# Four step tables of a four-layer transformer kernel in another order, with the waits that this order needs

## The reference

```python
mod = silu(cond) @ W_mod + b_mod                 # shift, scale, gate, twice
q, k, v = split((LN(x) * (1 + sc_a) + sh_a) @ W_qkv + b_qkv)
x = x + gate_a * (attend(q, k, v) @ W_proj + b_proj)     # self attention, 256 keys
x = x + attend(LN(x) @ W_q, context @ W_kv) @ W_cproj    # cross attention, 120 keys
x = x + gate_m * (gelu((LN(x) * (1 + sc_m) + sh_m) @ W_1) @ W_2)   # MLP, 1024 wide
```

## Time and profile before

| | before |
|---|---|
| median of three runs | 2457.98 us |
| profiled execution, its own time | 2459.47 us |
| its span, first to last instruction | 2457.7 us |
| TensorE (PE) busy | 2394.8 us, 97% |
| VectorE (DVE) busy | 1875.6 us, 76% |
| ScalarE (ACT) busy | 1263.5 us, 51% |
| GpSimd (POOL) busy | 466.9 us, 19% |
| chain that ended last | PE 91%, DVE 5%, ACT 1%, issue 1%, DMA 1% |

### The profile page before, as it was taken

The page is one execution under the profiler, slowest core; times in us unless marked ns, Lnnn a source line. Parts: engine busy times, 40 slices in busy tenths (PEclk is TensorE's granted clock), DMA queues, the critical chain, the costliest instruction groups (busy, mean ns, idle before and its releaser), DMA issues.

```text
span 2457.7 us, 93436 instructions
## 1 busy us (share of the span) xinstructions
PE 2394.8 (97%) x41326; PEld 1616.7 (66%) x41326; DVE 1875.6 (76%) x3532; ACT 1263.5 (51%) x1810; POOL 466.9 (19%) x510
## 2 busy tenths in 40 slices
...
GB/s 214 133 113 61 99 86 78 78 88 85 80 84 84 91 93 76 93 89 72 70 88 60 85 78 55 88 88 70 94 108 60 106 70 76 100 60 89 85 40 39
DMA packets 143669, 209.27 MB, mean 85 GB/s; under 512 B 14978, under 2 KB 75588, under 8 KB 143268
## 3 DMA queue, kind: packets, MB, share of 16 engines
...
...
## 4 chain that ended last, share of the span: by engine, by line
PE 91%; DVE 5%; issue 1%; ACT 1%; DMA 1%; SPq 0%; POOL 0%; POOLq 0%; DVEq 0%; ACTq 0%
PE ring L1220 38%; PE ring L1216 13%; PE o_acc L1380 12%; PE score L1327 11%; PE score L1349 9%; PE ring L1174 4%; PE score L1354 3%; DVE row_max_F L1008 3%; DVE row_max_G L1008 2%; ACT probs L1147 1%; DMA gate_now_P<-gate_rows 0%; SPq L693 0%; PE ring L1256 0%; DMA q_F<-q_parts 0%; DMA k_G<-k_parts 0%
## 5 line engine op out<-in xcount | busy, mean ns | idle before, releaser
L1147 ACT ACTIVATE probs<-score 120x2048 f32<-120x2048 f32 (+1 forms) x320 | 601.6, 1880 | 302.2 <-PE score L1354 273.5
L1008 DVE TENSOR_REDUCE row_max_F<-score 128x8 f32<-128x2048 f32 x192 | 438.6, 2285 | 88.8 <-PE score L1327 86.2
L1158 ACT ACTIVATE h_t<-ring,cols 128x256 f32<-128x256 f32 x384 | 160.6, 470 | 415.5 <-PE ring L1220 289.3
L1008 DVE TENSOR_REDUCE row_max_G<-score 128x16 f32<-128x1920 f32 x128 | 276.2, 2158 | 65.4 <-PE score L1327 65.4
L1220 PE MATMUL ring<-x_t_E,w_fc 128*32 128x256 f32 x4736 | 279.6, 380 | 0.0
L1030 DVE STREAM_TRANSPOSE o_turned<-o_acc 128x512 f32<-128x512 f32 x224 | 159.4, 712 | 127.7 <-PE o_acc L1380 127.2
L1220 PE MATMUL ring<-w_fc,h_t 128*32 128x256 f32 x3680 | 215.4, 380 | 0.0
L1220 PEld LDWEIGHTS ring<-x_t_E,w_fc 128*32 128x32 f32 x4736 | 149.0, 110 | 100.2
L1380 PE MATMUL o_acc<-probs,v_self 128*17 128x256 f32 x3072 | 203.8, 383 | 0.4 <-DVE o_turned L1030 0.4
L817 POOL TENSOR_TENSOR x<-x,gated 128x512 f32<-128x512 f32 x48 | 61.2, 1274 | 612.1 <-DVE gated L1049 611.8
L1349 PE MATMUL score<-q_F,k_F 32*128 32x256 f32 x3072 | 166.1, 302 | 9.0 <-ACT probs L1147 4.5
...
## 6 DMA issues: line engine op xcount, KB each, us to landing
k_F<-k_parts SPq DMA_DIRECT2D x192, 256.0 KB, 2.5
q_G<-q_parts SPq DMA_DIRECT2D x128, 256.0 KB, 2.6
k_G<-k_parts SPq DMA_DIRECT2D x256, 120.0 KB, 2.1
...
```

The lines of the kernel that those rows point to most:

```text
L1008: nc.vector.tensor_reduce(dst, src, AX.X, ALU.max).then_inc(row_max_ready[r].sem, 1)
L1147: nc.scalar.activation(probs[v % 2][0:keys, :, :], score[0:keys, :].rearrange("p (h q) -> p h q", h=2 * GROUPS), ACT.Exp, scale=SCALE).the ...
L1158: last = nc.scalar.activation(h_t[:, c, :], ps[:, c % 2 * NT:(c % 2 + 1) * NT], ACT.Gelu_apprx_tanh, bias=col(m, "fc1", c))
```

## The change

The four tables get another order. No step is added or taken away, no table takes a turn more or less, and no instruction changes its shape but for the products that change between untiled and four column tiles, since the steps around them changed. Two waits are added, because two orders are now possible that were not before: ACT waits for the Q, K and V products of the job before (not V alone) before it overwrites `x_t_P`, and PE waits for `x_t_P` before V too (until now V always stood behind a step that had waited).

```diff
 TURN = """
-F.S1 E.H1 P.V
-F.S2 E.H2 P.LN P.V.d
-F.S3 A.PR A.PR.d F.X E.H3
-G.S0 F.M B.PR R.C B.PR.d
...
+F.S1 E.H2 R.C P.LN P.gld
+F.S2 f.O1 f.PV3 P.V
+F.S3 F.X E.H3 A.PR P.V.d
+G.S0 c.ld A.PR.d F.M B.PR
...
 WITH_L1 = """
-1G.T0 R.N P.Q.d E.F21a G.M p.N
-1G.T1 1G.PV0 e.N 1G.O0 1R.KV R.RES
-F.T0 1G.PV1 1G.O1 E.F21b
+1G.T0 E.F21a P.K.d R.N G.M e.N R.A
+1G.T1 P.RES P.Q.d 1G.PV0 E.F21b p.N
+F.T0 1G.O0 1G.PV1 1R.KV
...
 START = """
-F0.T2 W0.v2 F0.PV1 P2.Q.d F1.X Z2.ZG F1.M P0.gld
+F1.S2 Z2.ZA F0.M P0.gld P2.Q W0.proj Z2.ZL Z2.ZS1
...
@@ block.scalar, step LN
                     if r == "P":
+                        q_psum[r].wait_before(act, m, n)
+                        k_psum.wait_before(act, m, n)
                         v_psum.wait_before(act, m, n)
@@ block.tensor, step V
                     if n == 0:
                         pe.wait_ge(w_v_loaded, full_done(m))
+                    pe.wait_ge(x_t_ready[r].sem, x_t_ready[r].after(m, n))
```

More of the change, by code:

```diff
@@ L49 @@
 TURN = """
-F.S0 f.O1 f.PV3 E.H0
-F.S1 E.H1 P.V
-F.S2 E.H2 P.LN P.V.d
-F.S3 A.PR A.PR.d F.X E.H3
-G.S0 F.M B.PR R.C B.PR.d
[L55 to L61, removed]
+F.S0 E.H0 E.H1
+F.S1 E.H2 R.C P.LN P.gld
+F.S2 f.O1 f.PV3 P.V
+F.S3 F.X E.H3 A.PR P.V.d
+G.S0 c.ld A.PR.d F.M B.PR
```

139 lines of the change are left out of this document (72 added, 67 removed).

## The result

The changed kernel takes 2462.58 us, the median of 18 runs (2458.76 to 2466.24). The kernel before, measured with it, takes 2458.17 (18 runs, 2456.30 to 2460.32). The ratio is 1.0016, its 95% interval 1.0010 to 1.0023: slower by 2.5 to 5.7 us, which is real but for the most part under the 4.9 us that counted as "slower" in the prediction. Of the kernels further down, `v2_early`, `best3` and `fx_pad` each had one execution that took 1.9 to 3.3 times as long as the others; it is counted in their medians and not in their ratios.

A forecast was written before the change was run, and what follows sets the result against it. PE was taken to bound the long middle, with idle time to gain only in the beginning. Terms 5.5 + 0.2 + 2.2 - 2.6 + 0.8 = +6.1 us on 2459.47 gave 2465.6, for a median 2464; range 2454 to 2472.

The forecast's parts named there:

- TURN, +5.5: 25 turns of `TURN`: +0.22 us each from PE's own work and waiting, +5.5 us in all (+2.5 to +9).
- edit 1: TURN: `R.C` leaves the interval behind `G.S0`; PE's own work +0.07 us a turn, plus a 0.09 us wait.
- The price of 1.98 for `B.PR`: TURN, `G.S0` interval: without `R.C`, untiled `B.PR` is followed by row tiles and takes 1.98 us, not 1.73.
- edit 2: TURN: new order of `R.LN`, `F21b`, `E.LN` before `F.T2`; 2.80 against 2.75 us, taken as +0.06 a turn.
- `G.PV0`: TURN: it moves by an interval, at a cost taken as 0 us, bounds -0.1 and +0.1.
- the thin covers: TURN: two covers under 0.1 us, as for PE's `F.T3`; taken as 0. Failing every turn: 2469, chance 0.15.
- Turns 3 to 5, +2.2: Turn 4: `F21b` leaves the `F.T0` to `F.T1` interval, PE idles, +1.9 us; with small shifts +2.2 (0 to +4.5).
- START, -2.6: First score step to turn 3: gate wait gone -2.4, other -0.5, later first score step +0.3; -2.6 us (-8.5 to +1.5).
- `P0.gld`'s early place on SP: START: the gate load stands four score steps earlier on SP, so DVE's wait at the first `A.PR` goes, some 2.4 us.
- `F.X` short in every job: `F.X`'s adding operation at 192 ns, not 1276, giving DVE 1.1 us a turn; pays nothing by itself.
- TAIL, +0.8: TAIL: two intervals fall under their need and others lose a little, +0.8 us (-0.5 to +2).
- The two intervals under their need: TAIL: `F15.S2` with one product, 2.5 against 3.15 us, and `G13.S1` with `KV` alone, 2.8 against 3.38.

The follow-up runs named there:

- v2_early: The kernel before with one START load, `W0.v2` (384 KB with its bias), moved to the beginning: 2454.71 us, ratio 0.9986.
- best3: The changed kernel with the old TURN, `E.F21b` behind `F.T0` in turn 4 and `P.Q` behind `F.T0` in turn 3: 2454.15 us, ratio 0.9980.
- fx_pad: The changed kernel with eight additional small DVE operations inside `F.X` in turns 22 to 46: 2461.53 us, ratio 1.0011.
- gld_late: The changed kernel with `P0.gld` moved back behind `F0.O0` in START, four score steps later: one run of 2459.67 us.
- fx_long: The changed kernel with `A.PR` and `A.PR.d` put ahead of `F.X` in TURN: 2486.12 us, ratio 1.0114.

## Why the prediction was right, and where its steps were not

The forecast, slightly slower, came out, with 2462.6 for 2464. That it came so near is luck in part. Measured in the two traces its terms add up to +2.3 us and not to +6.1: the loss in `TURN` was put 2.5 too high, that in the last turn 1.8, and the gain in `START` 1.1. Of the signs it named, the turn of 45.3 us, the short `F.X`, the 2.96 us with a hole in turn 4 and the first `A.PR` without a gate wait are there; turn 3 begins 1.5 us earlier and not 2 to 3.

- **TURN, +5.5, measured +3.0.** What held: there was no gain to be had from waits, and the `G.S0` interval lost its cover. The split was wrong. The prediction let edit 1 cost 0.07 of PE's own work and 0.09 of waiting. In the traces it costs PE no work, and 0.11 us of time because of two intervals that stand at their need. The `G.S0` interval needs 3.44 and not the 3.38 of the earlier trace rows (in turn 3 of before it takes 3.44 too, with 1.97 of waiting in it), so taking `R.C` out of it saved nothing; and the interval that took `R.C` in had 0.11 to spare for its 0.21, which the step left out. The price of 1.98 for `B.PR` in front of row tiles was misread: that interval of the earlier trace rows begins with an F `S` step at 691.42, so it is 3.15 long, which is its need, and 0.1 or more of the 1.98 is waiting.

```profile
691.42 0.75 PE L1327 MATMUL score<-k_F,q_F 32*128 32x256 f32 x16
```

  Where nothing waits, an untiled product takes 1.82 in front of row tiles (turn 4 of after, 199.50 to 201.32) and 1.72 in front of transposes (200.70 to 202.42 in before), and two transposes 0.32 (202.42 to 202.74 in before) and 0.22 (199.28 to 199.50 in after). So the way to row tiles costs 0.10 behind either. (Both are read in front of `T` steps. In front of an `S` step the product takes 1.87 in `fx_pad`, in an interval at its need, so a little of that can be waiting.) The rule of the Trainium skill that a change of mode drains TensorE ("TensorEngine Tiling (Array Packing)", Key Properties) would have made edits 1 and 2 free at one price for all changes. The trace agrees for edit 1. It disagrees for edit 2: the `LN` order cost 0.05 to 0.06, as the prediction said. `G.PV0` cost nothing, and the thin covers held. In sum 0.15, where 0.22 was forecast.
- **Turn 35**, which no term contains, gives 0.65 back. Turn 35 took 45.98 in before and 45.33 in after; five executions with the old table took 45.35 to 46.41, all those with the new one (but for the kernels that wait in every turn) 45.33. Why, stays open.
- **Turns 3 to 5, +2.2, measured +2.0.** Turn 4's hole was forecast at 1.9 and is worth 1.73; that the low clock might follow was its upper bound, 4.5, and it came in half of the executions. That the sum is near is luck: in these two traces the 2.33 of low clock in turn 4 met the 1.7 that turn 3 gained, and this gain can't be parted from `START`'s.
- **START, -2.6, measured -1.5 with the time to the first score step.** The wait of the earlier trace rows went and was worth 2.2 to 2.3 us against the trace of before, 1.2 to 1.6 against the two others with late weights. The reason given, `P0.gld`'s early place on SP, was not needed: in `gld_late` the load is late and in time, and with the 384 KB of `W0.v2` out of its way it is in time in the old order as well. The prediction counted the queue by who waits and not by bytes. With turn 3 the gain is 3.4.
- **`F.X` short in every job**, right; that its time covers `P.V.d` and pays nothing else, right as far as `fx_pad` goes. The port rule that the prediction drew on from the Trainium skill ("SBUF — State Buffer", Who interferes with whom) agrees: 192 to 197 ns for all 48 once POOL's add is elsewhere, and 1.28 us in `fx_long`, where it stands beside that add again (1397.65 and 1397.69).
- **TAIL, +0.8, measured -1.0.** Mis-sized. The two intervals under their need are there, with 0.54 and 0.44 us of waiting. But before lost 1.1 us at `G15.S0` on a `k_G` transfer, which no floor contains, and without it the last turn would have grown by 0.1; where the other 0.7 was won is not traced. To the end of the span the last turn took 130.1 to 130.6 us in the three executions with the old table, and with the new one 129.6 in eight of eleven and up to 130.7.

The two traces alone say +2.3 us, the medians +4.4. The profiled run of before lies 1.3 us over its median of 2458.17, that of after 0.8 under its own. So 2.1 of the 4.4 us are in no line of the account by stretches.
